# One program per engine across four graph layers, with the mask of one more attention head on GpSimd

## What is computed

```
x = layernorm(x + L0(x, adj))   # GAT, 8 heads of 16: leaky_relu(e1_i + e2_j), masked softmax, attn @ Wh
x = layernorm(x + L1(x, adj))   # GAT, 1 head of 128, then elu
x = layernorm(x + L2(x, adj))   # relational: relu(adj^T-weighted sum of (xW + b) * sigmoid(g + bg))
x = layernorm(x + L3(x, adj))   # attention, 4 heads of 32: softmax(Q K^T / sqrt(32)) under the mask, @ V, @ Wo^T + bo
```

## Time and profile before

| | |
|---|---|
| median of 3 runs | 851.84 us (847.98 to 851.87) |
| the profiled execution: its own time | 851.46 us |
| its span | 845.6 us |
| L0, first hidden matmul to last statistics | 24.4 to 293.6 us |
| L1, first normalize to last statistics | 300.6 to 458.3 us |
| L2, likewise | 465.2 to 572.0 us |
| L3, first normalize to last result | 576.7 to 837.1 us |
| verdict | 840.4 to 843.9 us |
| busy share of the span | PE 84%, DVE 73%, ACT 67%, POOL 47% |

### The profile page before, as it was taken

The page is one execution under the profiler, slowest core; times in us unless marked ns, Lnnn a source line. Parts: engine busy times, 40 slices in busy tenths (PEclk is TensorE's granted clock), DMA queues, the critical chain, the costliest instruction groups (busy, mean ns, idle before and its releaser), DMA issues. The chain is left out here.

```text
span 845.6 us, 26213 instructions
## 1 busy us (share of the span) xinstructions
PE 708.5 (84%) x8450; PEld 521.7 (62%) x8482; DVE 618.2 (73%) x1758; ACT 563.5 (67%) x1266; POOL 399.7 (47%) x615
## 2 busy tenths in 40 slices
PE   5589999999998467877872899995999999999992
PEld 3456666666665345655651799983666666667661
DVE  4168778778787537888887488885677777877865
ACT  1346666666665368888882899974777787777771
POOL 0447777878777313433432111112545555455540
PEclk9999999999998959999997799997999999999996
DMA  1523333333321022222220333321222222222211
GB/s 46 143 49 93 95 94 76 80 92 93 93 57 40 1 31 26 27 31 32 25 31 0 88 86 83 84 60 19 33 58 43 51 55 56 45 54 50 58 45 38
DMA packets 34919, 47.76 MB, mean 56 GB/s; under 512 B 4394, under 2 KB 18484, under 8 KB 34868
## 3 DMA queue, kind: packets, MB, share of 16 engines
q0 software_dynamic: 18576, 21.01, 15.6%
q1 hardware_dynamic: 16292, 26.10, 9.8%
HBM read 51.33 MB, written 8.39 MB: 71 GB/s over the span
## 5 line engine op out<-in xcount | busy, mean ns | idle before, releaser
L490 DVE SCALAR_TENSOR_TENSOR pp<-banks,floor,adj 128x1024 f32<-128x1024 f32 x128 | 157.3, 1249 | 2.9 <-PE banks L585 2.5
L1110 POOL TENSOR_TENSOR pp<-pp,adj 128x512 f32<-128x512 f32 x64 | 73.5, 1166 | 119.0 <-ACT pp L1151 119.0
L416 ACT COPY rows<-banks 128x640 bf16<-128x640 bf16 x64 | 44.3, 692 | 70.5 <-PE banks L562 70.3
L585 PE MATMUL banks<-pp,yv 128*17 128x128 f32 x2048 | 82.9, 281 | 1.5 <-DVE pp L490 1.4
L716 POOL TENSOR_TENSOR yres<-oo,x 128x512 f32 (+1 forms) x32 | 40.7, 1273 | 91.6 <-DVE oo L818 91.6
L1151 ACT ACTIVATE pp<-banks,nobound 128x512 f32<-128x512 f32 x128 | 81.5, 696 | 2.9 <-PE banks L1333 1.3
L572 PE MATMUL banks<-rows 32*128 32x128 bf16 x1024 | 51.8, 221 | 21.4 <-DVE pp L490 19.7
L1029 PE MATMUL banks<-w2b,xt 128*128 128x256 f32 x256 | 62.4, 388 | 0.0
L340 POOL TENSOR_TENSOR yv<-wh,yv 128x512 f32<-128x512 f32 x32 | 35.2, 1099 | 52.3 <-ACT yv L409 52.3
L913 POOL DMA_DIRECT2D adj<-in_adj x32 | 17.0, 533 | 86.1 <-ACT sq L948 75.1
L421 ACT COPY ot<-banks 128x512 f32<-128x512 f32 x64 | 37.4, 584 | 28.4 <-PE banks L585 28.4
(11 more groups left out here) (219 smaller groups left out, 1953.6 us busy)
## 6 DMA issues: line engine op xcount, KB each, us to landing
adj<-in_adjt POOLq DMA_DIRECT2D x96, 128.0 KB, 3.0
xt<-in_xt SPq DMA_DIRECT2D x32, 256.0 KB, 3.7
x<-in_x SPq DMA_DIRECT2D x32, 256.0 KB, 3.2
adj<-in_adj POOLq DMA_DIRECT2D x32, 256.0 KB, 3.0
out_ngd<-yres SPq DMA_DIRECT2D x32, 256.0 KB
w3q<-in_wq SPq DMA_DIRECT2D x1, 64.0 KB, 1.9
w3k<-in_wk SPq DMA_DIRECT2D x1, 64.0 KB, 1.8
ident<-in_ident SPq DMA_DIRECT2D x1, 64.0 KB
```

The source lines that it names most:

```text
L416: nc.scalar.copy(rows[:, slot % 2, a, :], R[:, 0:5 * N]).then_inc(s["rw"], 1)
L490: nc.vector.scalar_tensor_tensor(pp[:, g], S[g % 2][:, :].rearrange("p (h n) -> p h n", n=N), floor[:, slot:slot + 1], adj[:, slot, g:g + ...
L585: ins = nc.tensor.matmul(O[32 * h:32 * h + w, c:c + N], yv[:, slot % 2, g * H + 4 * half + h, :], pp[:, g, 4 * half + h, :], start=True, s ...
L1110: nc.gpsimd.tensor_tensor(pp[:, slot % 2, h], pp[:, slot % 2, h], adj[:, slot], ALU.mult).then_inc(s["pm"], 1)
```

## The change

The four layers, the row statistics and the verdict become one block: each engine has one program, in which the layers follow one another, with no barrier and no clearing of semaphores in between (`layers`). The layer functions now return a `Programs` object that holds one function for each engine. SBUF tiles are put at fixed offsets by `Plan`, so that tiles of neighbouring layers that are alive together don't overlap.

`Rows` replaces `row_statistics`. It works in two portions: the first 30 tiles, and the last two. `variance` (DVE), `roots` (ACT: Exp(-0.5 * Ln(v)) in place of Sqrt and the DVE reciprocal) and `refine` (DVE: one Newton step and nmr) are put among the last instructions of a layer and the first of the next. The last statistics of L1 and the last finish and statistics of L2 move behind the first normalize of the next layer. POOL issues the first adj loads of the next layer before its last residual of the present one.

The table set for Ln and Exp is loaded once at the head of L0. In L1 the order within a step changes on ACT and PE. In L3 POOL masks heads 0, 1 and 2, PE masks only head 3, and the third Exp is put ahead of `evac_xt`.

Changes of indentation are left out of this diff.

```diff
+class Rows:
+    def variance(self, dve, portion):
+        nc, c = self.nc, self.columns(portion)
+        me, ve, mo, vo = (self.stats[:, c, n] for n in (1, 2, 4, 5))
+        mean, d, v = self.mean[:, c], self.d[:, c], self.v[:, c]
+        nc.vector.tensor_tensor(mean, me, mo, ALU.add).then_inc(self.link, 1)
+        nc.vector.tensor_tensor(d, me, mo, ALU.subtract).then_inc(self.link, 1)
+        nc.vector.tensor_tensor(v, ve, vo, ALU.add).then_inc(self.link, 1)
+        dve.wait_ge(self.link, 8 * portion + 3)
+        nc.vector.tensor_scalar(mean, mean, 0.5, None, ALU.mult)
+        nc.vector.scalar_tensor_tensor(d, d, 0.25, d, ALU.mult, ALU.mult).then_inc(self.link, 1)
+        nc.vector.tensor_scalar(v, v, 1.0 / D, EPS, ALU.mult, ALU.add).then_inc(self.link, 1)
+        dve.wait_ge(self.link, 8 * portion + 5)
+        nc.vector.tensor_tensor(v, v, d, ALU.add).then_inc(self.var, 1)
+    def roots(self, act, portion):
+        act.wait_ge(self.var, portion + 1)
+        nc.scalar.activation(self.rstd[:, c], self.v[:, c], ACT.Ln).then_inc(self.log, 1)
+        act.wait_ge(self.log, portion + 1)
+        nc.scalar.activation(self.rstd[:, c], self.rstd[:, c], ACT.Exp, scale=-0.5).then_inc(self.root, 1)
+    def refine(self, dve, portion):
+        dve.wait_ge(self.root, portion + 1)
+        nc.vector.scalar_tensor_tensor(d, r, -0.5, r, ALU.mult, ALU.mult).then_inc(self.link, 1)
+        dve.wait_ge(self.link, 8 * portion + 6)
+        nc.vector.tensor_tensor(d, d, v, ALU.mult).then_inc(self.link, 1)
+        dve.wait_ge(self.link, 8 * portion + 7)
+        nc.vector.scalar_tensor_tensor(r, d, 1.5, r, ALU.add, ALU.mult).then_inc(self.link, 1)
+        dve.wait_ge(self.link, 8 * portion + 8)
+        nc.vector.scalar_tensor_tensor(self.nmr[:, c], self.mean[:, c], -1.0, r, ALU.mult, ALU.mult).then_inc(self.done, 1)
...
 multi, ACT and DVE
+        nc.scalar.preload_act_table_set("natural_log_exp_and_others")
         for n in range(3):
             copy_we(n, 0, n)
...
         evac_turned(T - 1, (T - 1) % RING, 0)
+        after.roots(act, 0)
         evac_turned(T - 1, (T - 1) % RING, 1)
...
+        dve.wait_ge(s["stats"], T - 2)
+        after.variance(dve, 0)
         statistics(T - 2, (T - 2) % RING)
+        after.refine(dve, 0)
         invert(T - 1, (T - 1) % RING)
         statistics(T - 1, (T - 1) % RING)
+        dve.wait_ge(s["stats"], T)
+        after.variance(dve, 1)
...
 single, POOL
+        pool.wait_ge(layer0.projected, 2 * T)
         for n in range(3):
             load_adj(n, n)
+        layer0.tail()
...
 single, ACT
         def evac_xt(n, slot):
             need(act, s["xt_tr"], n + 1)
-            need(act, s["we"], n - 1)
+            need(act, s["ab"], n - 1)
...
         normalize(0, 0)
-        evac_xt(0, 0)
         normalize(1, 1)
-        row_exp(0, 0)
+        evac_xt(0, 0)
         column_exp(0, 0)
+        row_exp(0, 0)
+        before.roots(act, 1)
         evac_xt(1, 1)
         normalize(2, 2)
-        normalize(3, 3)
-        row_exp(1, 1)
         column_exp(1, 1)
-        evac_xt(2, 2)
+        row_exp(1, 1)
+        normalize(3, 3)
         def step(t, slot, lap):
+            evac_xt(t + 2, ...)
             elu(t - 1, (slot - 1) % R8)
-            row_exp(t + 2, ...)
+            normalize(t + 4, ..., 0, 2)
             column_exp(t + 2, ...)
-            normalize(t + 4, ...)
-            evac_xt(t + 3, ...)
+            normalize(t + 4, ..., 2, NG)
+            row_exp(t + 2, ...)
...
         elu(T - 1, (T - 1) % R8)
+        after.roots(act, 0)
...
 single, DVE
         values(0, 0)
         weights(0, 0, 0)
+        before.refine(dve, 1)
...
+        dve.wait_ge(s["stats"], T - 2)
+        after.variance(dve, 0)
         elu(T - 1, (T - 1) % R8)
         statistics(T - 2, (T - 2) % R8)
+        after.refine(dve, 0)
+        def last():
             statistics(T - 1, (T - 1) % R8)
+            dve.wait_ge(s["stats"], T)
+            after.variance(dve, 1)
...
 single, PE
         def expand(n, slot):
             need(pe, s["xt"], n + 1)
-            need(pe, s["p"], n - 1)
-            nc.tensor.matmul(AB[slot % 2][:, :], k["wa1rep"][:, :], xt[:, slot % 2, :], ...).then_inc(s["ab"], 1)
             need(pe, s["y"], n)
             need(pe, s["bc"], n)
             for g in range(NG):
                 ins = nc.tensor.matmul(WE[:, g, :], xt[:, slot % 2, g * N:(g + 1) * N], k["w1e"][:, :], ...)
             ins.then_inc(s["we"], 1)
+            need(pe, s["p"], n - 1)
+            nc.tensor.matmul(AB[slot % 2][:, :], k["wa1rep"][:, :], xt[:, slot % 2, :], ...).then_inc(s["ab"], 1)
...
 relational, ACT and DVE
         evac_xt(1, 1)
+        before.roots(act, 1)
         tanh(0, 0)
...
         steps(act, step, 26, R8)
+        after.roots(act, 0)
...
-        for n in range(3):
-            normalize(n, n)
+        normalize(0, 0)
+        layer1.last()
+        normalize(1, 1)
+        normalize(2, 2)
         values(0, 0)
+        before.refine(dve, 1)
         def step(t, slot, lap):
+            if known(t) and t == T - 1:
+                dve.wait_ge(s["stats"], T - 2)
+                after.variance(dve, 0)
...
+        after.refine(dve, 0)
+        def last():
             finish(T - 1, (T - 1) % R8)
             statistics(T - 1, (T - 1) % R8)
+            dve.wait_ge(s["stats"], T)
+            after.variance(dve, 1)
...
 heads, POOL
-            need(pool, s["pm"], 2 * (n - 3))
+            need(pool, s["pm"], 3 * (n - 3))
...
             mask(t, 0, slot)
             mask(t, 1, slot)
+            mask(t, 2, slot)
             biased(t, slot)
...
 heads, ACT
             exps(t, 0, slot)
             exps(t, 1, slot)
+            exps(t, 2, slot)
             if not known(t) or t + 2 < T:
                 evac_xt(t + 2, (slot + 2) % RING)
-            exps(t, 2, slot)
             exps(t, 3, slot)
...
 heads, DVE
         normalize(0, 0)
+        layer2.last()
         normalize(1, 1)
...
 heads, PE
-            for h in range(2, H):
+            for h in range(3, H):
                 need(pe, s["p"], H * (n - 1) + h + 1)
                 nc.tensor.matmul(S[h][:, :], far[:, :], nota[:, slot % 2, :], start=True, stop=False, ...)
...
             need(pe, s["p"], H * (n + 1))
-            need(pe, s["pm"], 2 * (n + 1))
+            need(pe, s["pm"], 3 * (n + 1))
...
-        phase(multi, ...)
-        phase(row_statistics, 0, stats, mean, rstd, nmr)
-        phase(single, ...)
-        phase(row_statistics, 1, stats, mean, rstd, nmr)
-        phase(relational, ...)
-        phase(row_statistics, 2, stats, mean, rstd)
-        phase(heads, ...)
-        phase(verdict, ...)
+        phase(layers, fast, pb, k, c, yres, stats, rall, rec1, adjbad, rsum, flag, out_ngd)
```

More of the change, by code:

```diff
@@ L272, in multi @@
     end = 26
[L274 to L367, removed]
-                in2 = not known(t) or t + 2 < T
-                if in2:
-                    load_adj(t + 2, a2)
-                    high(t + 2, a2)
-                if not known(t) or t + 1 < T:
-                    values(t + 1, a1)
-                if in2:
-                    low(t + 2, a2)
-                if not known(t) or t >= 1:
-                    divide(t - 1, c0)
-                    residual(t - 1, c0, lap - (1 if slot == 0 else 0))
-            steps(pool, step, end)
@@ L689, in single @@
+    return block
+def single(nc, sb, sem, pb, k, yres, stats, before, after, rec, layer0, adjt):
     w, R8 = D + 1, 8
@@ L734, in normalize, with _ @@
+    @block.scalar
+    def _(act):
+        def normalize(n, slot, first=0, last=NG):
+            if first == 0:
+                if known(n):
+                    act.wait_ge(before.done, 1 if n < T - 2 else 2)
                 need(act, s["y_out"], n - 5)
-                for g in range(NG):
-                    at = n * NG + g
-                    ins = nc.scalar.activation(xr[:, slot, g, :], flat(at), ACT.Identity, bias=nmr[:, bass.ds(at, 1)], scale=rstd[:, bass.ds(at, 1)])
+            for g in range(first, last):
+                at = n * NG + g
+                ins = nc.scalar.activation(xr[:, slot, g, :], flat(at), ACT.Identity, bias=before.nmr[:, bass.ds(at, 1)], scale=before.rstd[:, bass.ds(at, 1)])
+            if last == NG:
@@ L772, in step @@
-            def step(t, slot, lap):
-                if not known(t) or t >= 1:
-                    elu(t - 1, (slot - 1) % R8)
-                if not known(t) or t + 2 < T:
-                    row_exp(t + 2, (slot + 2) % R8)
-                if not known(t) or t + 2 < T:
-                    column_exp(t + 2, (slot + 2) % R8)
-                if not known(t) or t + 4 < T:
-                    normalize(t + 4, (slot + 4) % R8)
-                if not known(t) or t + 3 < T:
-                    evac_xt(t + 3, (slot + 3) % R8)
@@ new lines, in elu, with step @@
+        def elu(n, slot):
+            need(act, s["o"], n + 1)
```

(35 more changed lines are left out.)

1759 lines of the change are left out of this document (945 added, 814 removed).

## The result

The changed kernel takes 943.96 us (median of 4 runs, 940.61 to 946.33) against 850.84 for the kernel before: 1.110 times as long, with a 95% interval of 1.105 to 1.114. The forecast of 829 us with a range of 812 to 842 was wrong, in size and in sign. The profiled execution after took 943.25 us, with a span of 938.7.

The account below looks back on a forecast made before the run. It took PE as L2's bound, a serial ring with no full engine in L1, PE apparently in L3, and pauses plus half clock at joins. Terms summed to -22.3 us from 851.5, giving 829, range 812 to 842.

Parts of the forecast that it names:

- The head of L0: L0's first table load, 1.28 us, moves to where ACT waits for weights and x: -1.3 us, or 0 if already covered.
- the port lock: Rival in L3: DVE holds up each of POOL's three masks over the shared port; slower at 857 us, chance 0.05.
- L1's order: New ACT and PE order in L1's step: period from 4.54 to 3.80 us, DVE the bound, -20.0 us.
- The joins: Earlier first normalizes between layers: -5.5 us from L0 to L1, -3.0 from L1 to L2, -2.0 from L2 to L3.
- Not all of the 9.1 is kept: L0 to L1: of a 9.1 us head start only 5.5 counts, the clock staying down until some 313 us.
- the clock stays up: Rival at the joins: shorter PE pauses, so the clock doesn't fall; 7.5 us more gained, 822 us, chance 0.12.
- The end: Verdict follows the results at once: 3.3 us less, 0.8 left for a longer clearing of semaphores, so -2.5 us.
- The third mask: L3's third head on POOL: three masks lengthen the tile from 7.60 to 7.95 us, +12 us with friction.
- The ring: L3's chain from attend through Ln, first Exp and three masks to the next attend: 7.95 us a tile.
- the Exps stand behind Ln and Exp of the denominators: L3, ACT's queue: 1.65 us from Ln to first Exp, so a quicker PE doesn't bring the Exps forward.
- Lock: Rival in L3: a mask waits for DVE's normalize or result on most tiles, 0.4 us each; +12, 841 us, chance 0.11.

Follow-up runs that it names:

- f1: Changed kernel plus one line in L2's ACT program, loading the Ln and Exp table set again behind L2's last check: 812.81 us, ratio 0.953.
- f4: Kernel before the change, without the one line that loads the Ln and Exp table set at L3's head: 986.10 us, ratio 1.158.
- k1: f1 with L1's order within a step and L3's masks both as before the change: 828.40 us, ratio 0.972.
- h1: f1 (three masks on POOL) with the Exp of the denominators moved behind the next tile's first head's Exp: 834.74 us, ratio 0.982.
- h2: f1 with two masks on POOL, L3's old Exp order, and the denominators' Exp moved behind the next tile's first head's Exp: 839.96 us, ratio 0.987.

## Why the prediction was wrong

**The step that failed is "The head of L0"**, with the words that the table load "moves to a point where ACT waits". I priced the preload by the one load that goes away from L0's ramp (1.3 us), and never asked what its place at the head of L3 had kept away; the 128 loads of L3 stood in the sum at nothing. The groups of the trace of the kernel before had the answer: one load at L943, L2's tanh, one at L1171, L3's head, and none in the 32 tiles of L3, although they hold Ln and Exp. So the set named there served both. Tanh displaces it: in the changed kernel the roots' Ln and Exp have no load ahead of L2's Tanh and one each behind it. With the line gone from L3, each Ln and each Exp there got a load of its own, 128 in all; which set each of them brought in, no trace says. f1 (one line, -131 us) and f4 (one line, +134 us in the other kernel) show it from both sides. That was no rival in the forecast, and for the slower side I had named the port lock.

The other terms, against the runs with the set kept:

- *L1's order*: -20.0 forecast, -23.0 measured. The steps are 3.67 us, where I had 3.68 as the bound and took 3.80; DVE has no wait left. The mechanism was right, and the discount for engines that don't mesh was not needed.
- *The joins, with the head and the end*: -1.3 - 5.5 - 3.0 - 2.0 - 2.5 = -14.3 forecast, -23 measured. By k1's rows the head starts were right, 9.0 for 9.1, 5.8 for 5.8 and 3.7 for 3.1; the wrong step is "Not all of the 9.1 is kept", and its like at L2. At L3 it was right, and too weak: 1.1 of the 3.7 was kept, for 2.0. I had the clock come back at the moment at which it did before (313.5), so that an earlier start would only put more work at half clock. It came back sooner by about as much as the ramp began sooner (11.4 for 11.7 us, 2.7 of both from L0), and 9.0 + 5.8 were kept where I had 5.5 + 3.0. The rival "the clock stays up" had nearly this time for these two joins, by a mechanism that did not happen: the clock fell at each of them.
- *The end*: it gave 3.4 for 3.3, and the 0.8 that I had left for a longer clearing was not needed: verdict and what follows it in the span take 6.1 us for 5.2, but the execution outside the span 4.6 for 5.9.
- *The head of L0, as far as L0 goes*: the 2.7 us in L0, where I had 1.3 for the table load, are not the load: L0's first attends are 0.3 sooner (46.4 for 46.7). Its last ones start at 284.3, 286.7 and 287.0 in k1, f1 and the kernel before, and the clock makes that difference. 2.0 of the 2.7 is one dip near the end of L0 in the profiled execution of the kernel before (266 to 272 us, granted clock 0.50; 1.00 in k1), and f1 is 2.3 later than k1 since L0's ramp, where its attends stay at 1.05 us longer before they drop to 0.63. L0's program is the same in f1 and k1, so such differences are of the execution, and those 2.7 of the 23 are not shown to be the joins'.
- *The third mask*: +12 forecast, +6.8 measured, 7.82 a tile for 7.95. The ring and its parts were right; 0.12 of the 0.13 was ACT's step from Ln to the first Exp (1.53 for 1.65). The 0.05 for the semaphore had no row behind it; in f1 it is 0.06 (660.56 to 660.62). PE's wait before attend is 0.23 us, not 0.5. That "the Exps stand behind Ln and Exp of the denominators" is what h1 and h2 probed, and the one move tried made another ring longer.
- *Lock*: DVE was held up by POOL, as the earlier trace rows had it, for some 1.5 us a tile, which leaves it busy 7.26 of 7.78 us (7.1 of 7.95 forecast), and POOL never by DVE for long enough to show in the masks (median 1.15 us, longest 1.24). The Trainium skill (SBUF — State Buffer, "Who interferes with whom") has either side block; here the trace agrees for DVE's side.

Put together without the loads: 851.9 - 23.0 - 23 + 6.8 = 813, as f1 has it. That is inside the stated range, but at its lower edge, and 16 us below the forecast, so the sum was off without the loads too, and the other way: 9 us at the joins, 5 at the mask and 3 in L1. The loads add 131.

The Trainium skill bears on the missed step too: "ScalarE: Activation LUTs", "Table sets: the hidden batching unit", lists tanh with the sets of exp and of sigmoid, and names only exp and ln for `natural_log_exp_and_others`, without giving the rest of that set. The load at L1027 agrees with tanh being outside it. The section also counts one load for an Ln followed by an Exp. The trace doesn't agree: without the named preload each of the two had a load, 32 times over. The same page of the Trainium skill, "What ACT_TABLE_LOAD costs", has about 1283 ns for a load, which agrees with each row above, and a further drain of about 1380 ns, which no row shows: the next instruction starts 0.01 or 0.02 us behind the load.

## What to carry to other kernels

A line that sets a state (a table set, a mode, a register) is priced by everything downstream that relied on it, not by its own duration: before moving one, list what else changes the state on the way, and count the loads in the inner loop. Follow every ring of a tile, not the tightest alone: in f1 the ring through the masks took 7.78 us, DVE was busy 7.26 of them and PE's projection began right behind DVE's divide, and moving one instruction by one place made another ring the longest. And put a cost where the engine waits anyway: the same load cost 1.23 us a tile, or next to nothing.

## What the runs showed that I had not expected

- A named preload changes what is loaded later: with it behind the last Tanh, Ln and Exp alternate in 32 tiles without a load; without it, 4 x 32 loads of 1.28 us.
- A table load costs no more than its row of 1.28 us: one more on the ring was 1.23 us a tile (852.07 - 812.81, over 32).
- One program in place of barriers, clearing of semaphores and whole row statistics at three joins and the end saved 23 us of 852. The stretch at the 1.2 GHz level behind a pause moves with the pause: at the first two joins the clock was back 11.4 and 18.2 us sooner, with a ramp that began 11.7 and 17.3 sooner.
- Full ACT makes PE dip: in L3 with the loads, the granted clock was 0.93 over 70 us and 0.90 over 120 (f4), and tiles with and without a dip alternate: 12.55 and 11.35 us, and 12.95 and 10.99 in f4.
